# Feed-forward by blocks of 512 tokens, with the projections, the norm work and the turned probabilities moved to shared PSUM banks

## The reference

```
mean, var = over features
x  = (x - mean) * rsqrt(var + eps) * weight + bias
x  = (x + tanh(cond @ lin_w.T + lin_b)) * weight + bias
h  = gamma(cond) * rmsnorm(x) + beta(cond)
q, k, v = h @ W_q.T, h @ W_k.T, h @ W_v.T          # 16 heads of 16
o  = softmax(scale * q k^T) v                       # within a sequence
x  = x + alpha(cond) * (o @ W_o.T)
h  = gamma'(cond) * rmsnorm(x) + beta'(cond)
x  = x + alpha'(cond) * (silu(h @ gate_w.T) * (h @ hidden_w.T) @ out_w.T + out_b)   # 1024 hidden
```

## Time and profile before

| | |
|---|---|
| median of 3 runs | 967.99 us |
| profiled execution | 969.26 us |
| its span, first to last instruction | 967.4 us |
| instructions in it | 28344 |
| TensorE matmul busy | 932.0 us (96%), 11164 products |
| VectorE / ScalarE / POOL busy | 717.1 (74%) / 616.8 (64%) / 582.4 us (60%) |
| mean granted TensorE clock | 0.993 |
| moved over the span | 23.33 MB, mean 24 GB/s |

### The profile page before, as it was taken

One profiled execution on the slowest core, in us unless ns is written; L12 is line 12 of the kernel. 1 busy time (PEld: TensorE's weight loads), 2 busy tenths in 40 slices (PEclk: granted clock), 3 DMA queues, 4 the chain that ended last, 5 costly groups with the idle time before them and its releaser, 6 DMA issues.

```text
span 967.4 us, 28344 instructions
## 1 busy us (share of the span) xinstructions
PE 932.0 (96%) x11164; PEld 896.9 (93%) x11164; DVE 717.1 (74%) x1355; ACT 616.8 (64%) x1732; POOL 582.4 (60%) x531
## 2 busy tenths in 40 slices
PE   5767999999999999999999999999999999999997
PEld 4757999999999999999999999999999999998997
DVE  5877787777878777777877777777777776677654
ACT  3566766766775766676676677667667666666432
POOL 4587657576674756757476675756666575544320
PEclk9799999999999999999999999999999999999999
DMA  7100010010000101010010101001000000000000
GB/s 228 57 2 24 2 32 16 13 34 13 24 13 14 34 13 35 2 35 13 13 34 14 34 2 35 13 13 34 13 23 13 13 13 12 13 13 13 13 12 22
DMA packets 20930, 23.33 MB, mean 24 GB/s; under 512 B 1216, under 2 KB 20288, under 8 KB 20800
## 3 DMA queue, kind: packets, MB, share of 16 engines
q1 hardware_dynamic: 20800, 21.54, 6.9%
HBM read 13.15 MB, written 8.39 MB: 22 GB/s over the span
## 4 chain that ended last, share of the span: by engine, by line
PE 91%; DVE 3%; POOL 2%; issue 2%; ACT 1%; DMA 0%; SPq 0%; DVEq 0%; ACTq 0%; POOLq 0%
PE psum L301 19%; PE psum L303 18%; PE psum L302 18%; PE psum L513 6%; PE psum L515 6%; PE psum L514 6%; PE psum L447 5%; PE psum L423 4%; PE psum L463 4%; PE psum L352 2%; PE psum L333 2%; PE psum L341 1%; PE psum L345 1%; POOL probs L1131 1%; DVE least L646 1%
## 5 line engine op out<-in xcount | busy, mean ns | idle before, releaser
L301 PE MATMUL psum<-xf_hi,ffn_hi 128*128 128x256 f32 x1024 | 289.7, 283 | 2.1 <-ACT probsT L929 1.8
L303 PE MATMUL psum<-xf_hi,ffn_lo 128*128 128x256 f32 x1024 | 286.0, 279 | 0.0
L302 PE MATMUL psum<-xf_lo,ffn_hi 128*128 128x256 f32 x1024 | 285.9, 279 | 0.0
L921 ACT ACTIVATE probs<-psum,least 128x64 f32<-128x64 f32 x928 | 206.3, 357 | 54.8 <-DVE least L646 54.1
L1131 POOL TENSOR_TENSOR probs<-probs,inv_sum 128x512 f32<-128x512 f32 x128 | 133.9, 1047 | 104.1 <-DVE inv_sum L667 103.4
L301 PEld LDWEIGHTS psum<-xf_hi,ffn_hi 128*128 128x128 f32 x1024 | 192.2, 188 | 3.3 <-issue 2.8
L303 PEld LDWEIGHTS psum<-xf_hi,ffn_lo 128*128 128x128 f32 x1024 | 192.4, 188 | 0.0
L302 PEld LDWEIGHTS psum<-xf_lo,ffn_hi 128*128 128x128 f32 x1024 | 192.0, 188 | 0.0
L950 ACT ACTIVATE prod_hi<-late 128x512 fp32r<-128x512 f32 x128 | 84.2, 658 | 115.1 <-DVE late L725 114.8
L513 PE MATMUL psum<-prod_hi,ffn_hi 128*128 128x256 f32 x512 | 143.3, 280 | 0.9 <-DVE prod_lo L731 0.9
L717 DVE SCALAR_TENSOR_TENSOR late<-tanh,psum 128x512 f32<-128x512 f32 x128 | 86.7, 677 | 76.9 <-ACT tanh L944 76.9
(11 more groups left out here) (103 smaller groups left out, 2207.0 us busy)
## 6 DMA issues: line engine op xcount, KB each, us to landing
out_t_dram<-x_res SPq DMA_DIRECT2D x31, 256.0 KB, 2.2
xin<-x_dram SPq DMA_DIRECT2D x15, 512.0 KB, 4.0
w_raw<-attn_w_dram SPq DMA_DIRECT2D x1, 1024.0 KB, 8.9
x_res<-gate_w_dram SPq DMA_DIRECT2D x1, 1024.0 KB, 11.5
late<-hidden_w_dram SPq DMA_DIRECT2D x1, 1024.0 KB, 13.0
w_raw<-out_w_dram SPq DMA_DIRECT2D x1, 1024.0 KB, 6.4
xin<-x_dram SPq DMA_DIRECT2D x2, 256.0 KB, 3.0
k_heads<-mod_w_dram SPq DMA_DIRECT2D x1, 320.0 KB, 4.0
```

What stands on the lines that cost most here:

```text
L301: pe.matmul(out, stat_hi, mov_hi, start=first, stop=False)
L302: pe.matmul(out, stat_hi, mov_lo, start=False, stop=False)
L303: return pe.matmul(out, stat_lo, mov_hi, start=False, stop=last)
L921: op = act.activation(probs[g % 4][:, h * SEQ:(h + 1) * SEQ], scores[g % 2][:, h // 2, h % 2], ACT.Exp, bias=least[g % 2][:, h:h + 1], sca ...
```

## The change

A feed-forward step makes 128 hidden features of a block of 512 tokens, where it made 256 features of a part of 256 tokens. There are 128 steps as before (`HT * NBLK`). A step's `gate`, `hidden` and `down` have 6 products of 512 columns each. The results of a block take two banks, 2 and 7. What used bank 7 moves: projections from slot 16 on, and the output projection, to the hidden half's bank (`proj_bank`); norm work to the gate's bank (`norm_bank(grp)`); turned probabilities to columns of the score banks that are free then (`turned_even`, `turned_odd`). Waits follow: projections wait for the last step's `product` (`hidden_bank_free`), norm work for the last `activate` (`gate_bank_free`), `gate` for norm work's readers, `hidden` for the projections' readers (`projection_read`), scores for both copies of turned probabilities. The tensor engine's list is written anew for slots from `FFN_AT` on: values, turned probabilities, x turned and projection, scores (behind the gate where j is 2), gate, hidden, down. `FFN_AT` is 16. VectorE takes `scale_a`, `scale_f`, `attended_lo` and `activate` ahead of `find_least` at j=2; `gate_ffn`, `add_ffn` and `store` work by blocks. `xf_hi` and `xf_lo` hold blocks; for the space, raw attention weights lie in `v_diag`, which is cleared after their split, and raw output weights in `late`, loaded at slot 5 in place of -3. The last step and the last down run by token halves.

```diff
-FFN_AT = 12
+FFN_AT = 16
-FFN_STEPS = 4 * NPART
+FFN_STEPS = HT * NBLK
-OUT_W_AT = -3
+OUT_W_AT = 5
...
-        gate_bank, hidden_bank, y_bank = bank[0], bank[1], bank[2]
-        norm_bank, work = bank[1], bank[7]
+        gate_bank, hidden_bank, y_bank = bank[0], bank[1], (bank[2], bank[7])
+        work = bank[7]
+        turned_even, turned_odd = psum[:, 3:7, 0:P], psum[:, 3:7, 3 * P:4 * P]
...
         def proj_bank(w, m):
-            return y_bank if m == 0 and w in (WQ, WV) else work
+            if not wide(PSEQ * (m - 1)):
+                return hidden_bank
+            return y_bank[0] if m == 0 and w in (WQ, WV) else work
...
+            def hidden_bank_free(s):
+                if s == FFN_AT:
+                    pe.wait_ge(gated_a_made, FFN_AT // PSEQ - 1)
+                else:
+                    pe.wait_ge(prod_made, s - FFN_AT)
+
+            def projection_read(s):
+                m, j = s // PSEQ + 1, s % PSEQ
+                if j < 3 and is_part(m):
+                    pe.wait_ge((k_out, q_out, v_out)[j], m + 1)
+                if j == 3 and is_part(m - 2):
+                    pe.wait_ge(gated_a_made, m - 1)
...
+            def score_banks_free(s):
+                if is_seq(s - 1):
+                    pe.wait_ge(scores_read, s)
+                if is_seq(s - 2) and not wide(s):
+                    pe.wait_ge(probsT_out, s)
...
+            def gate(f):
+                gate_wait(f)
+                up(gate_bank, 0, f, slice(0, BLK)).then_inc(gate_mm, 1)
+
+            def hidden(f):
+                hidden_wait(f)
+                up(hidden_bank, 1, f, slice(0, BLK)).then_inc(hidden_mm, 1)
...
+            def down_tile(f, mt, tok):
+                q = f % HT
+                cols = slice(q * D + mt * P, q * D + (mt + 1) * P)
+                return three_pass(y_bank[mt][:, tok], ffn_hi[:, 2, cols], ffn_lo[:, 2, cols], prod_hi[f % 2][:, tok],
+                                  prod_lo[f % 2][:, tok], q == 0, q == HT - 1 and tok.stop == BLK)
...
+            for s in range(FFN_AT, LAST_SLOT):
+                grp, j, f = s // PSEQ, s % PSEQ, s - FFN_AT
+                if s % 2 == 0:
+                    values_of(s)
+                    for g in (s - 2, s - 1):
+                        if is_seq(g):
+                            turn_probs(g)
+                if j == 0 and is_part(grp + 2):
+                    gate_bank_free(s)
+                    turn_x(grp + 2)
+                if j == 0 and is_part(grp + 1):
+                    keys(grp + 1)
+                if j == 0 and is_seq(s):
+                    scores_of(s)
...
+                if j == 3 and is_part(grp - 1):
+                    attention_out(grp - 1)
+                if is_step(f) and f < LAST_STEP:
+                    gate(f)
+                    if j == 2 and is_seq(s):
+                        scores_of(s)
+                    hidden(f)
...
+                if 1 <= f <= LAST_STEP:
+                    down(f - 1)
+            last_down()
...
+                if j == 2 and s >= FFN_AT and is_part(grp + 2):
+                    scale_a(grp + 2)
+                if j == 2 and s >= FFN_AT and is_part(grp - 2):
+                    scale_f(grp - 2)
+                if j == 2 and s >= FFN_AT and is_part(grp - 1):
+                    attended_lo(grp - 1)
+                if j == 2 and s >= FFN_AT and is_step(f):
+                    activate(f)
...
+                if f % HT == 1 and 0 <= f // HT - 1 < NBLK - 1:
+                    gate_block(f // HT - 1)
```

More of the change, by code:

```diff
@@ L368, in keys @@
                 pe.wait_ge(lo_a, m + 1)
-                if m >= 3 and not early_out(m - 3):
-                    pe.wait_ge(gated_a_made, m - 2)
+                if not wide(PSEQ * (m - 1)):
+                    hidden_bank_free(PSEQ * (m - 1))
                 elif m >= 2:
@@ L377, in queries @@
             def queries(m):
-                if m >= 1:
+                if not wide(PSEQ * (m - 1)):
+                    hidden_bank_free(PSEQ * (m - 1) + 1)
+                elif m >= 1:
                     pe.wait_ge(k_out, m + 1)
@@ L382, in values @@
             def values(m):
-                pe.wait_ge(q_out, m + 1)
+                if not wide(PSEQ * (m - 1)):
+                    hidden_bank_free(PSEQ * (m - 1) + 2)
+                else:
+                    pe.wait_ge(q_out, m + 1)
                 for t in range(2):
@@ L839, in _ @@
                     normalise_half(1, 1, 3)
-                if is_step(f):
-                    activate(f)
+                if j == 3 and is_part(grp - 2) and s >= BATCH:
+                    ffn_split_lo(grp - 2)
+                if is_step(f) and f < LAST_STEP:
+                    if j != 2:
+                        activate(f)
                     product(f)
-                if j == 3 and is_part(grp - 2):
+                if is_seq(s) and not wide(s) and s % 2 == 0:
+                    invert_sums(s)
+                if j == 3 and is_part(grp - 2) and s < BATCH:
                     ffn_split_lo(grp - 2)
@@ L944, in half_tanh, with tanh_last, product_hi_last @@
                 act.activation(tanh[:], gate_bank, ACT.Tanh, scale=0.5).then_inc(tanh_made, 1)
+            def tanh_last():
+                for u in range(2):
+                    act.wait_ge(gate_mm, LAST_STEP + 1 + u)
+                    if u == 0:
+                        act.wait_ge(act_made, LAST_STEP)
+                    act.activation(half(tanh, u), gate_out(LAST_STEP, u), ACT.Tanh, scale=0.5).then_inc(tanh_made, 1)
+            def product_hi_last():
+                for u in range(2):
+                    act.wait_ge(prod_made, LAST_STEP + 1 + u)
+                    if u == 0:
+                        act.wait_ge(out_mm, LAST_STEP - 1)
+                    act.activation(half(prod_hi[LAST_STEP % 2], u), half(prod, u), ACT.Copy).then_inc(prod_hi_made, 1)
             def product_hi(f):
@@ L1008, in _ @@
                     square_f(grp - 2)
-                if s % 2 == 0 and is_seq(s):
+                if s % 2 == 0 and is_seq(s) and wide(s):
                     exponentials(s)
@@ L1016, in _ @@
                         exponentials(s + 1)
-                if j == 0 and s >= 0 and is_part(grp + 2) and not PSEQ <= s <= FFN_AT:
+                if s == 0:
                     square_a(grp + 2)
@@ L1020, in _ @@
                     square_f(grp - 2)
-                if j == 2 and is_part(grp - 1) and not wide(s):
-                    attended_hi(grp - 1)
                 if j == 2 and PSEQ <= s < FFN_AT:
@@ L1045, in _ @@
                     values_out(1)
-                if is_step(f):
+                if is_step(f) and f < LAST_STEP:
                     half_tanh(f)
+                if s % 2 == 0 and is_seq(s) and not wide(s):
+                    exponentials(s)
+                if is_step(f) and f < LAST_STEP:
+                    product_hi(f)
                 if s % 2 == 0 and is_seq(s + 1) and not wide(s + 1):
                     exponentials(s + 1)
-                if is_step(f):
-                    product_hi(f)
                 for c in SPLITS.get(s, ()):
@@ L1148, in _ @@
                 grp, j, f = s // PSEQ, s % PSEQ, s - FFN_AT
+                if s == FIRST_SLOT + 4:
+                    pool.wait_ge(w_lo_made, 4)
+                    pool.memset(v_diag[:], 0.0).then_inc(v_cleared, 1)
                 if s == 0:
@@ L1171, in _ @@
                     sum_squares_f(grp - 2)
+                if j == 0 and s > FFN_AT and is_part(grp + 2):
+                    sum_squares_a(grp + 2)
+                if j == 0 and is_part(grp - 2) and not wide(s):
                     apply_gamma_f(grp - 2)
```

360 lines of the change are left out of this document (201 added, 159 removed).

## The result

The changed kernel takes 1017.91 us (median of 4 runs, 1017.42 to 1018.40) against 967.88; the ratio is 1.0516 with an interval of 1.0502 to 1.0530. 956 was forecast, 937 to 982 as the range. The profiled execution has a span of 1016.6 us.

The account below looks back on a forecast made before the run. TensorE, busy 932 of 967.4 us, was taken to bound the kernel through matmul spacing in the long middle. Start 102.9, middle 777.3, tail 67.3 and end 8.1 gave a span of 955.6, forecast as 956 us, range 937 to 982.

Parts of the forecast that it names:

- The wide product: Feed-forward on TensorE: one 512-column product replaces two of 256 at 118 ns each, saving 20 ns per pair, 1.44 us per part.
- I take 216, nearest to the half-clock row: Price of a 512-column product: 216 ns, since 256 columns at half clock showed only their 213 ns stream.
- The two ends: Start and tail: feed-forward four slots later, slots 12 to 15 at 19.9 us, start 102.9, 16-slot tail 67.3, end 8.1.
- The end's 8.1 us: After the tail: last step by halves, wider additions and stores, 8.1 us as before, plus or minus 0.5.
- The stalls: Middle parts: new TensorE waits from shared banks, 0.9 us per part, bounds 0 and 1.8.
- Stall 0.5 on every part, the largest: End of slot j=2: `attention_out` waits for VectorE's `product`, 8.0 against 8.5 us from the slot's start.
- `token_stats` ahead 0.2 late, every other part: Slot j=3: hidden waits for `gate_attention` behind `product_lo`; with `token_stats` ahead, 0.2 us late every other part.
- Stall 0.1: Slot j=2: the gate waits for both VectorE scalings, ready at 3.5 us against 3.42, on every part.
- The 0.3 behind `gate_block`: Slot j=1, once per block: the next block's first `down` needs `gate_block`, which comes 0.3 us late, every other part.
- `make_residual` is done by then: Slot j=0: keys and scores lie between `turn_x` and the gate, so `make_residual` adds no wait.
- (b): Rival: bank waits around slots j=2 to j=3 make it slower than before, 981 us at 1.8 us per part; chance 0.23.
- (c): Rival: 512 columns priced by the column at 236 ns, nothing saved, 991 us; at 225 ns, 973 us; chance 0.10.

## Why the prediction was wrong

**The wide product.** The step that failed is "I take 216, nearest to the half-clock row". The row was read rightly (213 ns, the stream alone) and the conclusion was wrong: an addition that a product at half clock hides was taken to be hidden by any stream of 213 ns. At 2.4 GHz 512 columns stream 213 ns too, and 13 ns are paid on top. So the extra goes with the type and the granted clock and not with the length of the stream. In the full kernel it was 231, and the saving 3 to 5 ns a pair of 118 ns products: 6.8 us by one pair of kernels and 7.9 by the other, not 46. The price of a weight load that the prediction cites is not what the traces show for this type either: a load takes 188 ns in the stretch and 187 to 188 in the feed-forward of the kernel before, against 98 with bf16. The Trainium skill's N/2.4 + 2.5 ("TensorE: Matmul & The Clock Gate", "Back-to-back issue gap") is what bf16 does here (216 ns); no fp32r stretch does. Its sustained 131 ns at N=512 appears in no run.

**The two ends.** x of part 6 is turned at 103.1 us, and 102.9 was reckoned; that is luck. Slots 12 to 15 begin at 78.4 and not at 82.5, and they take 24.7 us and not 19.9. In them TensorE was 61% busy, and the granted clock stood at half from 90.9 to 97.7; it did so once more from 107.9 to 111.3, and the first tanh came at 110.2, not near 106. The late start as a whole was reckoned at 9.1 us (19.9 + 0.5 + 17.0 for four more tail slots, less 28.3 for a part of the middle), and by the medians it costs 13.1. The rest is not in the profiled executions, which stand 8.8 apart; the lower granted clock of the other executions points to where it is, and that is not shown. The end's 8.1 us came out.

**The stalls.** 0.9 us a part were reckoned. The difference between the changed kernel and the one with freed banks and moved list is 38.6 us, 1.4 a part over 28. Set side by side with that kernel, product by product in the middle, the changed one loses 0.48 and 1.57 us in turn at j=3, 0.29 at j=2 in every part, and 0.02 at j=0.

- "Stall 0.5 on every part, the largest", ahead of `attention_out`, did not come: `product` ends at 306.33, 8.4 us behind the slot's start as reckoned (8.5), but TensorE gets there at 306.62, 8.65 behind it and not 8.0.
- At j=3 "`token_stats` ahead 0.2 late, every other part" was 1.45 late by the starts, and 0.37 in the parts without. The reckoning had `product_lo` at 0.69 us, and it takes 1.46 there. That is an operation with both inputs in SBUF: in the changed kernel it takes 0.69 us in all 27 places where POOL stands still, and up to 1.77 beside POOL. `attended_lo`, which reads PSUM, takes 0.69 beside POOL as well. The kernel before had such a row already:

```profile
338.93 1.77 DVE L731 TENSOR_TENSOR prod_lo<-late,prod_hi 128x512 fp32r<-128x512 f32 x1
```

- At j=2 "Stall 0.1" ahead of the gate had the right place and is 0.29. The 0.3 behind `gate_block` did not come: that `down` takes 1.54 us, those at j=1 of the other parts 1.47.
- At j=0 "`make_residual` is done by then" was wrong: it ends at 318.10, and the gate starts 0.3 us late in the part shown, and 2.2 once the wait ahead of it was taken away. `merge_stats`, seven operations and 1.5 us at the end of every other j=3, and `ffn_split_lo` at 1.3 to 1.7 were not in the reckoning at all. In the kernel before, whose TensorE has no idle time in the middle, they delayed nobody.

**Where the 50 us went.** In steps that each rest on a pair of runs: late start +13.1 (980.2 against 967.1); the rest of the rewriting (the new order of TensorE's list, the work by blocks, VectorE's list with the three moves, the place of the turned probabilities), at narrow products and free banks, +5.9 (986.1 against 980.2); wide products -6.8 (979.3 against 986.1); the shared banks with VectorE's list as it stands +38.6 (1017.9 against 979.3). The sum is 50.8, the measured difference 50.0. The kernels with freed banks sum two halves of a result into one bank, with the same number of products. Against the forecast of 956 the time is 62 us longer: 39 from the price of the wide product, 13 from the stalls, 6 from the rest of the rewriting, which had been put at nothing, and 4 from the late start. Of the 38.6, moving three operations of VectorE gives back 24.2 with the banks shared, and freeing the banks 34.5 with the list kept. Together that is more than there is: both undo the same waits, for a reader of a bank that stands too far down VectorE's list. The projections' bank alone is worth 3.7 us.

**The rivals** were put as if only one could hold. (b), the banks, and (c), the price, both did. 956 + 25 + 35 by the prediction's own numbers is 1016. That this comes so near is partly luck: it holds 50 us of stalls where 38.6 were measured, and neither the rest of the rewriting nor the dearer start. The range ended at one of them alone.

No version tried beats the kernel before. Of those that compute everything the best is the late start alone with narrow products, at 980.2, and with wide products the one with three moves, at 993.7. What stays open: why the rest of the rewriting costs 5.9 us. The turned probabilities in the scores' banks can have a share in that at most, and were not tried by themselves; they lie there in the kernel with freed banks too, where TensorE has no idle time, so the 38.6 is not theirs. Open too is what makes a wide product 231 ns and a narrow one 118 in the full kernel.

## What to carry to other kernels

Where an engine without idle time is given banks to share, walk the reader's whole list in every slot, with all its small operations and with durations from the places where they collide, and not only the reader itself: what delayed nobody before is now ahead of TensorE. An overhead that vanished at half clock was there again in a longer stream at full clock; look for a second shape at the same clock, or measure. And when two terms of a sum are uncertain independently, the range has to hold both at once.

## What the runs showed of the hardware

In a stretch of its own an fp32r product with a new 128x128 weight tile costs its columns at 2.4 GHz plus 13 ns, from 256 columns up (120, 174, 227 ns), and 111 ns at 128; bf16 costs 109 and 216. In the full kernel 256 and 512 columns of fp32r take 118 and 231 ns. At half clock the 13 ns are not seen (427 ns at 512). Data, busy neighbours, the same weights again, several banks and met waits change nothing. Four fp32 transposes ahead of six wide products add 0.03 us, ahead of twelve narrow ones nothing. A VectorE operation of 128x512 with both inputs in SBUF takes 0.69 us alone and up to 1.77 beside POOL; `attended_lo`, with one input in PSUM, takes 0.69 beside POOL as well.
